# One decoder step with four layers: self-attention of layer 3 with unnormalised exponentials transposed, and layer 3's cross-attention on its values product

## The reference, cut to what matters

```python
H, D = 16, 32                                   # heads, width of a head
q = jnp.einsum('bsc,hcd->bhsd', xn, wq)
k = jnp.einsum('btc,hcd->bhtd', yn, wk)
v = jnp.einsum('btc,hcd->bhtd', yn, wv)
a = jax.nn.softmax(jnp.einsum('bhsd,bhtd->bhst', q, k) * D ** (-0.5), axis=-1)
if causal:                                      # the self-attention
    mask = (jnp.arange(t)[None, :] > jnp.arange(s)[:, None]).astype(a.dtype)
    a = a * mask
o = jnp.einsum('bhst,bhtd->bhsd', a, v)
```

## Time and profile before

| | us |
|---|---|
| median of 3 runs | 2544.62 |
| lowest, highest | 2543.07, 2545.36 |
| the profiled execution's own time | 2524.31 |
| its span, first to last instruction | 2522.6 |
| TensorE busy | 2047.2 (81% of the span) |
| VectorE busy | 1367.6 (54%) |
| ScalarE busy | 929.6 (37%) |
| GpSimd busy | 710.5 (28%) |

### The profile page before, as it was taken

How to read it: one execution, slowest core, us unless ns; L and a number is a source line. 1 busy time by engine, 2 the same in 40 slices (tenths; PEclk the granted TensorE clock), 3 DMA queues, 4 the chain that set the end, 5 groups by cost and what they waited for, 6 DMA issues and landing times. The chain is left out here.

```text
span 2522.6 us, 36317 instructions
## 1 busy us (share of the span) xinstructions
PE 2047.2 (81%) x11904; PEld 1504.7 (60%) x11904; DVE 1367.6 (54%) x3511; ACT 929.6 (37%) x1859; POOL 710.5 (28%) x1199
## 2 busy tenths in 40 slices
PE   5983974467867677999799979969898589999991
PEld 4661863354444454555455558846687378888991
DVE  4871006535745765888688847757636432222332
ACT  4220321112324346888688843232232112222230
POOL 0223011030130125777577751102330230000005
PEclk9995995578979789999999989979999699999995
DMA  2004531000011286333333430110000525555684
GB/s 87 1 1 150 167 104 28 13 13 14 1 19 12 82 216 165 85 85 85 86 65 92 97 108 11 28 36 1 1 13 1 193 104 175 175 175 175 215 287 115
DMA packets 171504, 219.20 MB, mean 87 GB/s; under 512 B 39911, under 2 KB 133540, under 8 KB 165184
## 3 DMA queue, kind: packets, MB, share of 16 engines
q1 hardware_dynamic: 163344, 196.65, 26.7%
q0 software_dynamic: 7264, 20.31, 2.5%
q10 hardware_dynamic: 720, 0.07, 0.0%
HBM read 171.13 MB, written 46.14 MB: 86 GB/s over the span
## 5 line engine op out<-in xcount | busy, mean ns | idle before, releaser
L2390 DVE TENSOR_REDUCE l3s_mx<-banks 128x1 f32<-128x1024 f32 x256 | 313.1, 1223 | 96.7 <-PE banks L2292 93.8
L2292 PE MATMUL banks<-l_stack 128*128 128x512 bf16 x1024 | 268.1, 385 | 44.1 <-ACT xn_tokens L2373 21.0
L1012 PE MATMUL banks<-l3f_xrt,l3f_w 128*128 128x256 f32 (+1 forms) x1536 | 277.9, 342 | 2.7 <-issue 1.5
L1012 PEld LDWEIGHTS banks<-l3f_xrt,l3f_w 128*128 128x128 f32 x1536 | 249.6, 192 | 29.1 <-issue 3.3
L1302 DVE TENSOR_SCALAR l3f_sg<-banks 128x256 f32<-128x256 f32 (+1 forms) x192 | 72.0, 375 | 287.5 <-PE banks L1012 287.5
L2273 POOL TENSOR_TENSOR xn_tokens<-xn_tokens,l3s_sm 128x1024 f32<-128x1024 f32 (+3 forms) x128 | 201.6, 1575 | 50.3 <-DVE l3s_sm L2397 49.2
L222 PE MATMUL banks<-ident,xn_tokens 128*128 128x128 f32 x320 | 64.7, 338 | 166.8 <-DVE xn_tokens L211 148.0
L2292 PEld LDWEIGHTS banks<-l_stack 128*128 128x128 bf16 x1024 | 80.8, 98 | 163.3 <-ACT xn_tokens L2373 52.6
L2373 ACT ACTIVATE xn_tokens<-banks,l3s_mx 128x1024 f32<-128x1024 f32 x128 | 142.7, 1115 | 46.2 <-DVE l3s_mx L2390 45.1
L222 PEld LDWEIGHTS banks<-ident,xn_tokens 128*128 128x128 f32 x320 | 46.6, 172 | 188.4 <-DVE xn_tokens L211 133.0
L2373 ACT ACTIVATE x_features<-banks,l3s_mx 128x1024 f32<-128x1024 f32 x128 | 143.0, 1117 | 27.9 <-DVE l3s_mx L2390 27.6
(11 more groups left out here) (532 smaller groups left out, 3925.4 us busy)
## 6 DMA issues: line engine op xcount, KB each, us to landing
l3f_w<-in_L_ffn_gate_up_w_dram SPq DMA_DIRECT2D x24, 2048.0 KB, 7.6
l3f_w<-in_L_ffn_down_w_dram SPq DMA_DIRECT2D x24, 1024.0 KB, 6.0
l_stack<-l_q_part SPq DMA_DIRECT2D x72, 256.0 KB, 6.0
l_stack<-l_k_part SPq DMA_DIRECT2D x72, 256.0 KB, 11.4
l0f_w<-in_L_ffn_W_dram SPq DMA_DIRECT2D x16, 1024.0 KB, 5.8
l_q_part<-l_stack SPq DMA_DIRECT2D x24, 256.0 KB, 3.0
l_k_part<-l_stack SPq DMA_DIRECT2D x24, 256.0 KB, 3.7
l3f_rows<-l3f_zero SPq DMA_DIRECT2D x13, 384.0 KB, 4.1
```

Of the source, the lines that this page charges most:

```text
L1012: last = nc.tensor.matmul(ps[:, f % 4, h * PAIR:h * PAIR + size], w1_sb[:, p, dc, h * FF + f * P:h * FF + (f + 1) * P], xrt[:, p, dc, 0:si ...
L2292: last = nc.tensor.matmul(ps[:, 2 * (v % 2) + h, :], stack[p][0][s][:, r, si * P:(si + 1) * P], stack[p][1][s][:, r, h * 512:(h + 1) * 512 ...
L2390: nc.vector.tensor_reduce(mx[:, v % RING:v % RING + 1], ps[:, 2 * (v % 2):2 * (v % 2) + 2, :].rearrange("p a n -> p (a n)"), AX_X, ALU.max ...
```

## The change

It is made in three places. The diff, cut to its core:

```diff
@@ stage_attention
-    narrow = width * 4 <= KEYS
+    narrow = width * 2 <= KEYS
@@ self_attention_scratch
-    parts = [[dram(f"l3_{kind}_part{m}", [ENTRIES + 1, P, TOK], BF16) for m in range(3)] for kind in ("q", "k")]
-    values = dram("l3_values", [ENTRIES + 1, P, KC, P], F32)
+    parts = [[dram(f"l3_{kind}_part{m}", [ENTRIES, P, TOK], BF16) for m in range(3)] for kind in ("q", "k")]
+    values = dram("l3_values", [ENTRIES, P, KC, P], F32)
@@ stage_self_project, sync
                     places = [(b * GROUPS, GROUPS)]
-                    if b == 0:
-                        places.append((ENTRIES, 1))
@@ stage_self_attention
-    BODY = 4
     RING = 8
-    TURN = 5
-    STORE = TURN
-    OUT = TURN + R + 1
+    TURN = 3
+    OUT = TURN + R + 2
...
+    SCORES = 3
+
+    uses, last_turn = {}, {}
+    for v in range(ENTRIES * UNITS + OUT):
+        if v >= OUT and (v - OUT) % R == 0:
+            uses["out", (v - OUT) // R] = len(uses)
+        if TURN <= v < ENTRIES * UNITS + TURN:
+            for g, group in enumerate(groups):
+                if group[0] == (v - TURN) % UNITS:
+                    uses["turn", (v - TURN) // UNITS, g] = len(uses)
+                    last_turn[(v - TURN) // R] = uses["turn", (v - TURN) // UNITS, g]
...
-        with nc.Fori(0, ENTRIES // BODY) as jj:
...
@@ sync
+                load_entry(sp, scratch, entry, 1, 1)
+                for e in range(ENTRIES):
+                    sp.wait_ge(out_ready, KC * (e + 1))
+                    if e + 2 < ENTRIES:
+                        load_entry(sp, scratch, entry, e + 2, e % 2)
...
@@ gpsimd
-                        pool.wait_ge(inverted, v + 1)
-                        nc.gpsimd.tensor_tensor(ex[v % RING][:, si * P:], ex[v % RING][:, si * P:],
-                                                sm[:, v % RING:v % RING + 1].to_broadcast([P, TOK - si * P]), ALU.mult)
-                        pool.drain()
...
+                def spread_inverse(w):
+                    pool.wait_ge(inverted, w + 1)
+                    if w >= 2:
+                        pool.wait_ge(out_ready, w - 1)
+                    nc.gpsimd.tensor_copy(spread_inv[:, w % 2], inv[:, w % 2, :].unsqueeze(2).to_broadcast([P, R, W])).then_inc(spread, 1)
+
+                def scale(w):
+                    e, si, n = w // KC, ORDER[w % KC], uses["out", w]
+                    pool.wait_ge(stored[n % 2], stored_through(n % 2, n))
+                    if e >= 2:
+                        pool.wait_ge(out_sent[e % 2], 16 * (e // 2))
+                    nc.gpsimd.tensor_tensor(heads_out[:, e % 2, si * P:(si + 1) * P], raw[:, w % 2, 0:P], raw[:, w % 2, P:2 * P],
+                                            ALU.mult).then_inc(scaled, 1)
+
+                for v in range(ENTRIES * UNITS + OUT + 2):
+                    if v >= R + 1 and (v - R - 1) % R == 0 and (v - R - 1) // R < ENTRIES * KC:
+                        spread_inverse((v - R - 1) // R)
+                    if OUT + 1 <= v <= ENTRIES * UNITS + OUT and (v - OUT - 1) % R == 0:
+                        scale((v - OUT - 1) // R)
...
+                    pool.wait_ge(exped, v + 1)
+                    nc.gpsimd.affine_select(out=ex[v % RING][:, si * P:(si + 1) * P], in_=ex[v % RING][:, si * P:(si + 1) * P],
...
@@ tensor
-                        if v >= 2:
-                            pe.wait_ge(exped, v - 1)
+                    if v >= SCORES:
+                        pe.wait_ge(exped, v - SCORES + 1)
...
+                def output(w):
+                    e, si = w // KC, ORDER[w % KC]
+                    n = uses["out", w]
+                    for side in range(2):
+                        pe.wait_ge(stored[side], stored_through(side, max(last_turn[w], n - 2 if side == n % 2 else 0)))
+                    for c in range(si, KC):
+                        for r in range(R):
+                            nc.tensor.matmul(ps[r * W:(r + 1) * W, 6 + n % 2, 0:P],
+                                             values[:, e % 2, c, r * W:(r + 1) * W],
+                                             pt[:, w % 2, r, c - si, :], start=(c == si),
+                                             stop=(c == KC - 1))
+                    pe.wait_ge(spread, w + 1)
+                    nc.tensor.transpose(ps[:, 6 + n % 2, P:2 * P], spread_inv[:, w % 2].rearrange("p r d -> p (r d)"),
+                                        core["ident"][:, :]).then_inc(out_ready, 1)
...
+                    if v < ENTRIES * UNITS:
+                        scores(v)
+                    if v >= OUT and (v - OUT) % R == 0:
+                        output((v - OUT) // R)
+                    if TURN <= v < ENTRIES * UNITS + TURN:
+                        turn(v - TURN)
+            def store_output(eng, op, v, side):
+
+                if not OUT <= v < ENTRIES * UNITS + OUT or (v - OUT) % R != 0:
+                    return
+                w = (v - OUT) // R
+                if uses["out", w] % 2 != side:
+                    return
+                eng.wait_ge(out_ready, w + 1)
+                if w >= 2:
+                    eng.wait_ge(scaled, w - 1)
+                dst, src = raw[:, w % 2, :], ps[:, 6 + side, 0:2 * P]
+                last = op.activation(dst, src, ACT.Copy) if side == 0 else op.tensor_copy(dst, src)
+                last.then_inc(stored[side], 1)
@@ scalar
+                for v in range(ENTRIES * UNITS + OUT + 1):
+                    store_output(act, nc.scalar, v, 0)
+                    if v >= TURN:
+                        store_turned(act, nc.scalar, v - TURN, 0)
...
@@ vector
+                for v in range(ENTRIES * UNITS + OUT + 1):
+                    store_output(dve, nc.vector, v, 1)
...
+                    if v >= TURN:
+                        store_turned(dve, nc.vector, v - TURN, 1)
+                    if R <= v <= ENTRIES * UNITS and v % R == 0:
+                        w = v // R - 1
+                        dve.wait_ge(exped, v)
                         if w >= 2:
+                            dve.wait_ge(spread, w - 1)
+                        nc.vector.reciprocal(inv[:, w % 2, :], sm[:, w % 2 * R:w % 2 * R + R]).then_inc(inverted, 1)
```

More of the change, by code:

```diff
@@ L2089, in sent_before @@
             def sent_before(k):
-                return sum(16 * 8 * (2 if q < PAIRS // B else 1) for q in range(k % 2, k, 2))
+                return sum(16 * 8 for q in range(k % 2, k, 2))
             @block.gpsimd
@@ L2225, in stage_self_attention, with stored_through, turned_through @@
     BANKFULS = len(groups)
-    assert BANKFULS % 2 == 0
-    def groups_through(u):
-        return sum(1 for g in groups if g[0] <= u)
+    SCORES = 3
[8 more added lines that the diff above has]
+                    last_turn[(v - TURN) // R] = uses["turn", (v - TURN) // UNITS, g]
+    def stored_through(side, n):
+        return (n + 2 - side) // 2
+    def turned_through(v):
+        return BANKFULS * (v // UNITS) + sum(1 for g in groups if g[0] <= v % UNITS)
     with ExitStack() as ctx:
@@ L2399, in stage_self_attention @@
-            clear_semaphores()
-        nc.sync.wait_ge(loaded[0], 16 * LOADS * (ENTRIES // 2 + 1))
-        nc.all_engine_barrier()
+                        n = uses["turn", e, g]
+                        if n >= 2:
+                            pe.wait_ge(stored[n % 2], stored_through(n % 2, n - 2))
+                        for c in range(size):
+                            last = nc.tensor.transpose(ps[:, 6 + n % 2, c * P:(c + 1) * P],
+                                                       ex[v % RING][:, (si + c0 + c) * P:(si + c0 + c + 1) * P],
+                                                       core["ident"][:, :])
@@ new lines, in turn @@
+                        last.then_inc(turned, 1)
+                def output(w):
[12 more added lines that the diff above has]
+                                        core["ident"][:, :]).then_inc(out_ready, 1)
@@ new lines, in _ @@
+                for v in range(ENTRIES * UNITS + OUT):
+                    if v < ENTRIES * UNITS and v % UNITS == 0:
+                        e = v // UNITS
+                        pe.wait_ge(loaded[e % 2], 16 * LOADS * (e // 2 + 1))
+                    if v < ENTRIES * UNITS:
[4 more added lines that the diff above has]
+                        turn(v - TURN)
@@ new lines, in store_turned @@
+            def store_turned(eng, op, v, side):
+                if v >= ENTRIES * UNITS:
+                    return
+                e, w = v // UNITS, v // R
+                for g, (u, c0, size) in enumerate(groups):
+                    if u != v % UNITS or uses["turn", e, g] % 2 != side:
+                        continue
+                    n = BANKFULS * e + g
+                    eng.wait_ge(turned, n + 1)
+                    if w >= 2:
+                        eng.wait_ge(out_ready, w - 1)
+                    dst = pt[:, w % 2, v % R, c0:c0 + size, :].rearrange("p c n -> p (c n)")
+                    src = ps[:, 6 + side, 0:size * P]
```

(5 more changed lines are left out.)

186 lines of the change are left out of this document (57 added, 129 removed).

## The result

The changed kernel takes 2501.95 us (median of 4 runs, 2500.86 to 2503.67) against 2543.85 for the kernel before it (4 runs on the same chip): a ratio of 0.9835, 95% interval 0.9818 to 0.9852. That is 41.9 us less, where 36.8 were forecast.

The account below looks back on a forecast made before the run. TensorE was taken to hold the self-attention body, with chains of waits close behind. Self-attention 30.3, projection 4 and cross-attention 2.5 sum to 36.8 us: 2544.6 - 36.8 = 2508 us, own range 2497 to 2520.

Parts of the forecast that it names:

- Loop's turn: Self-attention: the turn of the loop over entries goes with the loop, 15.4 us less.
- Pace: Self-attention body: time a unit falls from 1.888 to 1.83 us, 256 units then taking 468.5 us.
- TensorE's sum: Self-attention: TensorE's own work for a pair of tiles falls from 14.6 to 14.4 us, 1.80 a unit.
- slack rival: Self-attention: TensorE has slack the starts don't show; 1.74 us a unit, 23 us more gained, 2485; chance 0.14.
- The pace stays: Rival, self-attention: shared banks tie TensorE to ScalarE's copies, only the loop's turn goes there; 2523 us; chance 0.19.
- The output holds everything: Rival, self-attention: output copies at the head of a unit make TensorE stand still; up to 2562 us; chance 0.09.
- VectorE: Self-attention: losing 192 of 256 reciprocals, 29 us, and getting half of 64 output copies gains nothing, hidden by TensorE.
- Fill and drain: Self-attention's edges apart from the loop's turn: stay at 11.3 us, bounds 8 and 14.
- Projection: Fewer SyncE writes let the load of entry 0 move up: 4 us less, bounds 0 and 6.
- Cross-attention: Layer 3's cross-attention becomes narrow: 4.5 us less in folding weights, loop unchanged, pipeline 2 more; together 2.5 less.
- Clock: Rival, self-attention body: new waits lower the clock from 1.00 to 0.90, 51 us more, 2559; chance 0.03.
- Carry-over: Whole kernel: the runs' median lies 20.3 us above the profiled execution, and this difference stays after the change.

Follow-up runs that it names:

- first experiment: The kernel before the change, unchanged, run and profiled once more: 2541.83 us.

## Why the prediction was right, and where it was wrong

The time, 2501.95, is 6.1 under the forecast, inside its own range.

- **Loop's turn**: right as a mechanism, 12.9 to 14.4 measured alone for 15.4.
- **Pace**: 1.83 forecast, 1.826 measured, but by two errors that cancel, which is luck. The step that failed is TensorE's sum, "New sum 14.4, 1.80 a unit", with "This part is worth almost nothing". By the starts above the pair of tiles is 8 x 0.87 scores + 36 x 0.107 transposes + 2 x 0.13 + 9 x 0.22 output + 2 x 0.16 inverses + 2 x 0.09 where output follows scores = 13.55, 1.69 a unit. The 0.10 of a group of transposes was kept as a price of each of the eight switches, but in the earlier trace rows both groups stand ahead of an output, and it is the output's: 6.5 in a pair before, 2 now. Summed that way the kernel before has 8 x 0.87 + 36 x 0.107 + 6.5 x (0.09 + 0.14) + 9 x 0.22 = 14.3, 1.79 a unit, and 0.10 of waiting in its 1.888. Now the waits are not 0.03 but 0.08 to 0.14 (1.826 less 1.742, or less 1.69). So TensorE's work fell by 0.1 a unit and the waits did not fall with it: the third buffer took away the one that it was aimed at, the scores' for the exponential, and others, for banks that VectorE and ScalarE empty, took its place.
- **The slack rival** (1.74 a unit) came near the floor, though the 0.13 of an output piece stays. The argument against it, "the gaps stand in every switch of rows 4, and these stay", was the mistake. It failed in that the waits stayed. **The pace stays** fell. **The output holds everything** exists in small: the 1.56 above. How much of the 2578 with two buffers it is was not taken apart.
- **GpSimd**: "It was the pace of an eighth of the units" was wrong; taken away by itself, its work is worth nothing.
- **VectorE**: "nothing, and what hides it is TensorE" was wrong. In large tiles it needs as long as TensorE (1.73 each), and with its stand for the output ahead of them it is the later one; the run with half the maximum puts 21 to 24 us on it and on the length of the chain. An average of 83% busy hid that.
- **Fill and drain**: 8.1, the lower bound, for 11.3.
- **Projection**: 3.9 in the spans and 4 to 5.6 by the run with the writes put back, for 4; the wait 5.10 for "about 5".
- **Cross-attention**: 2.8 for 2.5, also with luck. In the loop the terms came one by one, 1.02 and 1.83 for 1.0 and 1.8, a wait of 1.28 for 1.3, but the loop and what follows it took 3.6 more where the forecast has 2, and ahead of the first scores it was 6.4 less for 4.5. The Trainium skill gives two-fold column tiling for a left side of 64 and four-fold for 32 (TensorEngine Tiling (Array Packing), When to Use Tiling). The trace agrees: 16 recorded products take 1.02 us here and 0.58 in layer 2's form.
- **Clock**: a granted clock of 1.00 in every stretch shown here, also with two score buffers, where the scores' loads waited 112 times in some 200 units. The switching between clock levels that the Trainium skill tells of (TensorE: Matmul & The Clock Gate, A second HAM failure mode: psum-queue depth-cycling) did not show in these stretches.
- **Carry-over**: right, and its cause is found (first experiment).

No kernel of this study that computes the whole is faster than the changed one.

## What to carry to other kernels

Before keeping a gap between two kinds of instructions as a price of every switch, look at which pairs of kinds show it: two rows that both stand ahead of the same kind say nothing of the others. When the profile names a releaser, compare its end with the start of what waited; here a copy that ended 0.12 us before was the releaser, and not the mask that was named. To know whether a 96% busy engine is the bound, shorten its busiest neighbour for one run, by leaving out a part of its work; busy time and moved waits both misled here. And balance engines per tile, by distances between starts, not on average, when the buffers are fewer than the units of a tile.

## What the runs showed of the hardware that was not expected

**A change of the left side's width costs 0.09 us each way.** From one transpose (128 columns on the left) to the next there are 0.11 us between starts, from a transpose to an output product (32 columns) 0.20; from the last of the scores to a transpose 0.22, to an output product 0.31. Back to 128 columns it is 0.20 too, and so on both sides of the 32- and 64-column products of the cross-attentions (L522). This holds in nearly every such place of the kernels before and after. At such a change the weight load starts with its product instead of ahead of it. The first two rows are such a place in the kernel before:

```profile
1073.18 0.16 PEld L2326 LDWEIGHTS banks<-l3s_pt,l_values_in 128*32 128x32 f32 x8 [0.17 <-issue]
1073.18 0.43 PE L2326 MATMUL banks<-l3s_pt,l_values_in 128*32 128x128 f32 x8
...
1074.42 0.82 PE L2308 MATMUL banks<-ident,xn_tokens 128*128 128x128 f32 x6
...
1075.15 0.55 PEld L2292 LDWEIGHTS banks<-l_stack 128*128 128x128 bf16 x4 [0.16 <-ACT x_features L2373]
1075.16 1.04 PE L2292 MATMUL banks<-l_stack 128*128 128x512 bf16 x4
```

In the changed kernel it still stands, ahead of 8 outputs in 32 units, where it stood ahead of 26 pieces: scores at 1108.43, output at 1109.39, whose load is listed at 1109.39 too. The other rows show a second cause: six transposes cost 0.74 there, because the next load waited for the exponential. In the changed kernel the scores' load starts 0.11 ahead of the product (1108.32 and 1108.43 above), and six cost 0.65.

**A wait of 20 to 26 us in the expert part** on VectorE, put down to "remote", is there in 13 of 14 profiles and absent in one. Whoever compares two single profiles would put it to the change. What it waits for was not tried.
